# Gate mean in two steps, count copies one tile later, first mix tile by blocks, in a graph transformer block

## What is computed

```python
xn = _layernorm(x)
x = x + gnn(xn, edges) + mix(xn)        # gnn: 2 layers of neighbour sums and products; mix: linear attention
x = x + ffn(_layernorm(x))

# mix
q = softmax(q, over the head's 64); k = softmax(k, over the rows); v = v / N
context = einsum('bnhd,bnhe->bhde', k, v); out = einsum('bhde,bnhd->bhen', context, q) ...
out = out @ w_out + b_out; out = layernorm(out) * ln_scale

# ffn, x is the normalised input
gh = relu(x @ gfc1_w.T + gfc1_b)
g = (gh @ gfc2_w.T + gfc2_b).mean(over the rows)      # 8 numbers
W1m = W1 + sum_e g[e] * tv_W1[e]; W2m = W2 + sum_e g[e] * tv_W2[e]
out = relu(x @ W1m.T + b1m) @ W2m.T + b2m
```

## Time and profile before

| | us |
|---|---|
| median of 3 runs | 495.91 |
| lowest, highest run | 491.88, 495.99 |
| profiled execution | 494.36 |
| its span, first to last instruction | 491.9 |
| mean granted TensorE clock in it | 0.981 of full |

### The profile page before, as it was taken

One profiled execution on the slowest core, in us unless ns is written; L12 is line 12 of the kernel. 1 busy time (PEld: TensorE's weight loads), 2 busy tenths in 40 slices (PEclk: granted clock), 3 DMA queues, 4 the chain that ended last, 5 costly groups with the idle time before them and its releaser, 6 DMA issues.

```text
span 491.9 us, 9954 instructions
## 1 busy us (share of the span) xinstructions
PE 455.7 (93%) x3600; PEld 356.5 (72%) x3600; DVE 306.5 (62%) x715; ACT 250.2 (51%) x529; POOL 164.7 (33%) x176
## 2 busy tenths in 40 slices
PE   1989999999999999998999999999999969989991
PEld 1877668886766676766999995679999858965650
DVE  4777798756999857855655349625333685523396
ACT  4789345146722355345344756425436377744463
POOL 1379552112083023033336890004232123312513
PEclk9999999999999999999999999999999969998997
DMA  8702002202020002011100001000000289930015
GB/s 249 218 3 79 8 0 88 87 1 85 1 88 0 2 3 85 1 69 44 63 0 0 1 2 62 1 0 1 0 1 5 85 190 214 213 69 1 3 53 156
DMA packets 7263, 27.46 MB, mean 56 GB/s; under 512 B 1260, under 2 KB 1385, under 8 KB 5816
## 3 DMA queue, kind: packets, MB, share of 16 engines
q1 hardware_dynamic: 7224, 26.92, 19.9%
HBM read 24.36 MB, written 2.56 MB: 55 GB/s over the span
## 4 chain that ended last, share of the span: by engine, by line
PE 82%; DVE 9%; ACT 3%; POOL 2%; issue 2%; DMA 1%; SPq 0%; DVEq 0%; ACTq 0%
PE ps L473 52%; PE ps L661 17%; PE ps L462 4%; PE ps L554 2%; POOL late L1737 2%; PE ps L757 2%; PE ps L564 1%; DVE r L1696 1%; DVE r L1684 1%; PE ps L459 1%; DMA x<-in_x 1%; DVE r L1204 1%; ACT r L843 1%; DVE late L1205 1%; DVE r L1677 1%
## 5 line engine op out<-in xcount | busy, mean ns | idle before, releaser
L473 PE MATMUL ps<-r,wslot 128*128 128x250 f16 x840 | 96.7, 274 | 2.9 <-DVE r L1204 2.7
L473 PEld LDWEIGHTS ps<-r,wslot 128*128 128x128 f16 x840 | 82.1, 99 | 15.2 <-DVE r L1204 4.4
L661 PE MATMUL ps<-late,r 125*128 (+1 forms) x800 | 87.1, 269 | 1.4 <-issue 1.4
L661 PEld LDWEIGHTS ps<-late,r 125*128 125x128 f16 x800 | 77.4, 97 | 11.3 <-issue 2.1
L1745 POOL TENSOR_TENSOR wslot<-stage,wslot 128x512 f16<-128x512 f32 x32 | 39.5, 1264 | 111.2 <-ACT wslot L809 111.2
L473 PE MATMUL ps<-wslot,r 128*125 128x512 f16 x300 | 68.8, 380 | 0.0
L473 PEld LDWEIGHTS ps<-wslot,r 128*125 128x125 f16 (+1 forms) x300 | 40.1, 136 | 21.2
L1779 POOL TENSOR_TENSOR late<-ohs,late 128x250 f16<-128x250 f32 x40 | 25.7, 652 | 86.7 <-ACT late L992 86.7
L473 PE MATMUL ps<-late,wslot 128*128 (+1 forms) x480 | 51.7, 269 | 0.0
L473 PEld LDWEIGHTS ps<-late,wslot 128*128 128x128 f16 x480 | 46.6, 97 | 5.3 <-issue 0.8
L473 PE MATMUL ps<-wslot,late 128*125 128x512 f16 x216 | 48.9, 380 | 0.2 <-DVE late L1496 0.2
(11 more groups left out here) (189 smaller groups left out, 709.6 us busy)
## 6 DMA issues: line engine op xcount, KB each, us to landing
late<-in_tv SPq DMA_DIRECT2D x16, 512.0 KB, 20.4
x<-in_x SPq DMA_DIRECT2D x5, 448.0 KB
out<-r SPq DMA_DIRECT2D x10, 224.0 KB
stage<-in_w_up SPq DMA_DIRECT2D x2, 1024.0 KB, 5.1
stage<-in_w_down SPq DMA_DIRECT2D x2, 1024.0 KB, 5.3
stage<-in_w_lin SPq DMA_DIRECT2D x1, 1024.0 KB, 6.1
stage<-in_w_k SPq DMA_DIRECT2D x1, 1024.0 KB, 4.9
stage<-in_w_q SPq DMA_DIRECT2D x1, 1024.0 KB, 4.9
```

The source lines that it names most:

```text
L473: last = nc.tensor.matmul(out, stat_(hs, b), mov(hm, b), start=start and n == 0, stop=stop and n == 3 * blocks - 1)
L661: last = nc.tensor.matmul(bank("t", m), u_nat[layer][:, p, h, m * 128:(m + 1) * 128], counts(h)[:, chunk], start=(start and h == 0 and p = ...
```

## The change

It has three parts. The gate mean: DVE sums the 19 finished columns of `gsum`, multiplies and adds while the last relu runs, then adds the last column in one step; the bias of the gate goes in as a fifth term of that sum (divided by 128, since ones over 128 partitions add it up), and the picks read PE's bank directly. The value stage: ACT copies window t-1 after value tile t, and window 9 at the end. The mix stage: tile 0 waits for m block by block instead of for all four.

```diff
@@ natural_tile, PE
-            def natural_tile(family, phase, mov, w, t, use):
+            def natural_tile(family, phase, mov, w, t, use, ready=None):
                 slot = use % RING[family]
                 wait_bank(pe, family, phase, use, slot)
-                passes(bank(family, slot)[0:P, :], ..., KB).then_inc(full[family], 1)
+                passes(bank(family, slot)[0:P, :], ..., KB, ready=ready).then_inc(full[family], 1)
@@ mix, PE
-            wait_done(pe, "z", "m", KB)
             for t in range(T):
                 wait_done(pe, "x", "qt", t + 1)
...
-                natural_tile("n", "mix", q_t, mm, t, t)
+                natural_tile("n", "mix", q_t, mm, t, t, ready=(lambda b: wait_done(pe, "z", "m", b + 1)) if t == 0 else None)
@@ value tiles, ACT
                     nc.scalar.activation(v_nat[:, 0, t, :], bank("z", i % 4)[0:P, :], ACT.Copy, scale=1 / S_W).then_inc(v_high, 1)
-                    window("v", t)
+                    if t:
+                        window("v", t - 1)
+            window("v", T - 1)
             split_weight("down0")
@@ gate, DVE
-            wait_done(dve, "t", "gate", 20)
-            then(nc.vector.tensor_reduce(gmean[:, :], gsum[:, :, :], AX.X, ALU.add))
-            then(nc.vector.scalar_tensor_tensor(g_terms[:, :, :].rearrange("p e k -> p k e"), gfc2[:, :, :], 1 / N,
+            nc.vector.tensor_scalar(g_last[:, :], gfc2[:, KB - 1, :], 1 / N, None, ALU.mult)
+            nc.vector.tensor_scalar(g_terms[:, :, KB], col("gfc2_b", 0, E), 1 / 128, None, ALU.mult)
+            wait_done(dve, "t", "gate", KB * J - 1)
+            nc.vector.tensor_reduce(gmean[:, 0:KB - 1], gsum[:, 0:KB - 1, :], AX.X, ALU.add)
+            then(nc.vector.tensor_reduce(gmean[:, KB - 1:KB], gsum[:, KB - 1, 0:J - 1], AX.X, ALU.add))
+            then(nc.vector.scalar_tensor_tensor(g_terms[:, :, 0:KB].rearrange("p e k -> p k e"), gfc2[:, :, :], 1 / N,
                                                 gmean[:, :].unsqueeze(2).to_broadcast([128, KB, E]), ALU.mult, ALU.mult))
-            nc.vector.tensor_reduce(g_part[:, :], g_terms[:, :, :], AX.X, ALU.add).then_inc(g_ready, 1)
+            then(nc.vector.tensor_reduce(g_part[:, :], g_terms[:, :, :], AX.X, ALU.add))
+            wait_done(dve, "t", "gate", KB * J)
+            nc.vector.scalar_tensor_tensor(g_part[:, :], g_last[:, :], gsum[:, KB - 1, J - 1:J], g_part[:, :], ALU.mult, ALU.add
+                                           ).then_inc(g_ready, 1)
             wait_full(dve, "x", "g", 0)
-            nc.vector.tensor_tensor(gcol[:, :], bank("x", 0)[:, 0:E], col("gfc2_b", 0, E), ALU.add).then_inc(g_col, 1)
-            dve.wait_ge(g_col, 1)
             for set_ in range(SETS):
-                last = nc.vector.scalar_tensor_tensor(g_picked[:, set_, :], gcol[:, GROUPS * set_:GROUPS * (set_ + 1)], 1.0,
-                                                      in_group[:, :], ALU.mult, ALU.mult, accum_out=g_own[:, set_:set_ + 1])
-            then(last)
-            for set_ in range(SETS):
+                then(nc.vector.scalar_tensor_tensor(g_picked[:, set_, :], bank("x", 0)[:, GROUPS * set_:GROUPS * (set_ + 1)], 1.0,
+                                                    in_group[:, :], ALU.mult, ALU.mult, accum_out=g_own[:, set_:set_ + 1]))
+                if set_ == SETS - 1:
+                    nc.vector.tensor_copy(gcol[:, :], bank("x", 0)[:, 0:E]).then_inc(g_col, 1)
                 nc.vector.tensor_scalar(g_stack[:, set_, :], of_group[:, :], g_own[:, set_:set_ + 1], None, ALU.mult
                                         ).then_inc(diag_ready, 1)
+            dve.wait_ge(g_col, 1)
@@ later on DVE
-            nc.vector.tensor_scalar(grow[:, :], bank("x", 1)[0:E, 0:P], cols[0:E, COL["gfc2_bc"][0]:COL["gfc2_bc"][0] + 1], None,
-                                    ALU.add).then_inc(g_vec, 1)
+            nc.vector.tensor_copy(grow[:, :], bank("x", 1)[0:E, 0:P]).then_inc(g_vec, 1)
```

## The result

| | before | after |
|---|---|---|
| median, 20 runs each on the same chips (us) | 495.7 | 491.27 |
| lowest, highest | 491.88, 498.55 | 490.01, 494.02 |
| profiled execution, its span | 494.36, 491.9 | 491.77, 489.4 |
| mean granted clock in it | 0.981 | 0.987 |

The ratio is 0.9941 with a 95% interval of 0.992 to 0.9962: 2.9 us faster, between 1.9 and 4.0, against the 1.6 forecast. The two medians lie 4.4 us apart, which is more than the gain: 8 of the 20 runs of before lie between 491.9 and 493.5 and 12 from 495.4 up, and the median falls into the second heap. A second comparison, on another chip, gave 0.9953 (0.992 to 0.9985). By the bound of 1% this is no change; it is a small gain, clear of noise.

What follows compares the result with a forecast made beforehand. TensorE was taken as the bound (busy 93% of the span, 82% of the chain of waits). Savings of 0.2 + 0.66 + 0.75 = 1.6 us take the median from 495.91 to 494.3 us; range 490.3 to 496.6.

Steps and rivals of the forecast that it cites:

- Value stage: Count copies one tile later on ACT bring the last window's register load forward: 0.2 us saved, bounds 0 and 1.3.
- The step that decided: End of value stage: the last register load must wait for window 8's issue, ending at 177.0, 0.2 us earlier than now.
- Rival C: Value stage: the register load follows the offsets, giving 1.3 us there, 2.7 in all, 493.2 us; chance 0.08.
- Mix tile: First mix tile starts one DVE subtraction earlier by waiting block by block: 0.66 us saved, bounds 0 and 0.66.
- the new waits hold nobody: First mix tile: the bank's wait covers blocks 0 to 2, and block 3 is ready long before its matmuls.
- Gate: Last gate sum to the merges: 0.46 us saved before the small matmul, 0.29 behind it, 0.75 together; bounds 0.4 and 0.8.
- the chain's releaser: Before the merges: the chain names the second stack as releasing PE; if so, the gate saving shrinks from 0.75 to 0.4 us.
- rival B: Clock drop at 442 us, after the gate, goes with PE's shorter pause: 1.6 + 1.14 us saved, 493.2 us; chance 0.18.
- A: The forecast itself, all three edits: 494.3 us, its own range 493.2 to 495.5; chance 0.52.
- D: Edits hardly take: value stage 0, mix gain given back, PE waits on second stack; 0.4 us saved, 495.5 us; chance 0.12.
- E: Slower: low clock after 397.7 us lasts 6.8 us longer into the gate product, costing 3.4, net 1.8, 497.7 us; chance 0.10.

## Why the prediction was right, and where it was off

**Value stage: 0.2 forecast, 0.15 measured.** The step that decided, that the register load stands behind window 8's issue and not behind the offsets, can be read directly. In after the offsets are written at 177.0 and the load starts at 178.4; the first row is the load line for windows 8 and 9, the second DVE's write:

```profile
L456 PEldq TENSOR_LOAD <-offsets x2: 1103/1103/1103, 175.2 to 178.4; - x2
```

```profile
L1192 DVE TENSOR_SCALAR offsets<-base x1: 155/155/155, 177.0 to 177.0; 1x16 int32<-1x16 f32 x1
```

The prediction's working gives the same: window 8's load ends at 176.3 here, 2.0 us of issue make it 178.3. Before it started with the offsets. The zero matmul behind the load comes 1.62 us after that of window 8, in before 1.72: 0.1 us earlier, and not 0.2. DVE ran ahead by the 1.3 us that were worked out (177.0 here is 175.8 on before's scale, where it was 177.05), and nearly all of it went into waiting for PE. Rival C is out. DVE's waits for the tile copy fell from 2.2 us to 1.1, not to nearly none: what is left is PE's own pace.

**Mix tile: 0.66 forecast, 0.46 measured.** The mechanism held; the term was mis-sized. The step was that the tile starts one subtraction earlier with nothing else in the way. What failed is the sentence that the new waits hold nobody: nobody waits for their condition, but the instructions themselves take time. Between the release and the first matmul PE now goes through two wait instructions where before it went through none, and the run with one wait shows what one takes, 0.1 us. PE's idle time fell from 0.90 to 0.43, not to 0.24.

**Gate: 0.75 forecast, 0.71 measured**, the same 0.71 with the edit alone. The bias, the fifth term and the picks from the bank cost nothing to be seen; the last DVE step took 0.24 instead of 0.20. PE starts the merges right after the first stack, before the second is written, so the chain's releaser in the earlier trace rows was a coincidence and 0.4 the wrong reading. Timeline of after:

```profile
439.69 0.24 DVE L1633 TENSOR_SCALAR ohs<-ohs 128x32 f32<-128x32 f32 x1
...
440.08 3.64 PE L757 MATMUL ps<-late,ohs 128*32 128x512 f32 x32 [0.32 <-DVE ohs L1633]
440.12 0.23 DVE L1633 TENSOR_SCALAR ohs<-ohs 128x32 f32<-128x32 f32 x1
```

The second stack is there 0.27 us after the first merge begins; PE wants it after 0.9.

**The sum.** 1.32 us of the three edits, 1.6 forecast. The 2.9 us of the comparison are more than that, and for two reasons.

The first is luck. The 20 runs of before in that comparison took 494.8 us on average, the 98 later ones 493.8; 12 of the 20 are above 495 us, and 29 of the 98. So about 1 us of the 2.9 is the draw of runs and chips. Against the 98, the mean span of after is 2.0 us lower (1.4 to 2.6), of which 1.3 to 1.5 are fixed.

The second may be rival B, which had a chance of 0.18. The drop after the gate is in none of the seven traces with the short pause, and kernels with the long pause had runs at 0.977 (27 of 98, 3 of 12, 2 of 12) where those with the short one had none (0 of 32 and 12). With a pause of 4.7 us no run stayed in the highest group. Against it stand the two traces with a pause of 2.7 and 2.9 us and no drop. So the link with the gate edit is likely from the counts, and how the pause brings it about isn't shown. Rival B priced the drop at 1.14 us for every run; the two profiles have 1.13. But only about half of before's runs (50 of 98 below 0.985) can have had it, which makes 0.6, and 0.5 to 0.7 of the mean is left for it. The step that failed here is that B was held apart from A as another outcome. It is a share of runs that adds to A; the sum would have been 1.6 + 0.5.
The Trainium skill, "TensorE: Matmul & The Clock Gate", Part 1, has it that the clock follows how busy PE has lately been and that the moment varies from run to run. The traces agree with the second: behind the same pause of 2.7 to 2.9 us the granted clock fell to about 0.5 in two traces and stayed at 1.00 in two.

**The median, 494.3 forecast, 491.27 measured**, is further off than the gain. The 495.91 of three runs was no bad anchor, since 20 runs gave 495.7. But both stand in the upper heap of before's runs, and after's 20 runs lie between 490.0 and 494.0 with no such heap, so that the median fell by 4.4 us. The measured median is below the 493.2 that A, B and C each had as their lowest; the stated range holds it only because it was carried down to the lowest run of before. That it came out right is in part luck.

**Rivals D and E** did not come: the mix turns stayed at 3.76 us, and the low stretch after layer 2 did not run into the gate product for longer. It was shorter, 6.8 us instead of 10.2, and the traces tell what that is worth. From the end of layer 2 to the second chunk of the gate product all eight traces with 6.8 us take 15.2 us, whichever edits they have, the three with 10.2 us take 16.1, the two without a low stretch 14.6, and the one with two of 3.4 us 15.6. The kernel before, filled only at the gate, shows both. First the one with 11 idle matmuls, 6.8 us low:

```profile
394.07 0.48 ACT r L1042
...
409.24 2.58 PE ps L473 x24
```

Then the one with 11 and 5, 10.2 us low:

```profile
393.57 0.48 ACT r L1045
...
409.70 2.57 PE ps L473 x24
```

So the 0.92 us of the table is the length of the low stretch and not an edit. It also corrects rival E's price: 3.4 us more at the low level cost 0.92 us and not 1.7, since PE doesn't bound all of this stretch. What decides the length stays open. The gate edit comes after it in an execution; yet the 10.2 us were seen only in three traces with before's gate part, and after's runs at 0.984 have no trace.

## What to carry to other kernels

Where PE's pause is followed by work that bounds the kernel, price it twice: its length, and the share of runs in which the clock is low after it. Where runs fall in groups, a difference of medians can be much larger than the gain; compare means over many runs, or spans at one mean clock, and look at the traces before taking a clock value for a pattern. When a producer is made earlier, ask what else the consumer's own instruction stream has to finish first: here 1.3 us of lead were worth 0.15. Work that is slow to issue, such as matmuls with addresses in registers, hides one by one between others, not as a block behind them.

## What the runs showed of the hardware

- A wait that is already fulfilled costs about 0.1 us on PE when it is an instruction of its own between the release and the next matmul (0.24 us with two, 0.14 with one, 0.04 with none).
- A block of 60 matmuls ahead of a register load does not hide the load: it started 2.5 us after the first of them, and the 15 matmuls after it took 1.72 us; spread between blocks of three they took 0.03 us each.
- The granted clock fell to 0.50 also at 181 us, behind the exposed last window of the value stage; it made 120 small matmuls 1.6 us longer (8.43 us instead of 6.80). Whether this happens changes from run to run of one kernel.
- Behind an unfilled pause of 2.7 to 2.9 us on PE the granted clock fell in two traces and not in two; where it fell, it was 5.3 us from the first merge to the first ffn product instead of 4.2.
- Keeping PE busy with idle matmuls behind layer 2 left no low stretch there and shortened it by 0.6 us in the traces (14.60 us instead of 15.18); over 12 runs no gain in time could be seen.
